# Moving more of the expert tiles and nine output groups into the main loop, and normalising the late groups on VectorE alone

## The reference

```python
x = x + gnn(layernorm(x), adj)       # 8192 rows of 128, adj 8192 x 8192
x = x + moe(layernorm(x))            # 16 experts, the best 2 of each row

def gnn(z, dist):                    # cutoff 1, mu 1, sigma 0.5
    weights = where(dist < 1, exp(-(1/dist - 1)**2 / 0.5), 0)
    return weights @ (z @ W + B)

def moe(x):
    topk_vals, topk_idx = top_k(x @ gate_w + gate_b, 2)
    share = softmax(topk_vals)
    expert_e(x) = relu(x @ w1[e] + b1[e]) @ w2[e] + b2[e]    # 128 -> 256 -> 128
    y = x + share[0] * expert_top1(x) + share[1] * expert_top2(x)
    return layernorm(y) * gamma + beta
```

## Time and profile before

| | before |
|---|---|
| median of three runs | 1727.93 us (1727.41 to 1729.02) |
| the profiled execution | 1725.96 us, its span 1724.2 us |
| busy, share of the span | PE 93%, ACT 91%, DVE 87%, POOL 31% |
| mean granted TensorE clock | 0.977 |
| first start of L720 in group 8 / 9 / 13 / 14 / 15 | 745.4 / 840.0 / 1243.0 / 1345.4 / 1453.6 us |
| last start of L720 (step 511) | 1553.4 us |
| last product of the tail | 1671 us |

### The profile page before, as it was taken

The page is one execution under the profiler, slowest core; times in us unless marked ns, Lnnn a source line. Parts: engine busy times, 40 slices in busy tenths (PEclk is TensorE's granted clock), DMA queues, the critical chain, the costliest instruction groups (busy, mean ns, idle before and its releaser), DMA issues.

```text
span 1724.2 us, 24880 instructions
## 1 busy us (share of the span) xinstructions
PE 1605.5 (93%) x8327; PEld 1069.9 (62%) x8327; DVE 1494.9 (87%) x2312; ACT 1563.5 (91%) x1530; POOL 538.3 (31%) x354
## 2 busy tenths in 40 slices
PE   4999999999999999999999999999998998988870
PEld 3666666666666666656666666666665665757760
DVE  7999989898989898999787878878898898877676
ACT  5899999999999999999999999999997998966662
POOL 1001040404040404090303012040464655465773
PEclk9999999999999999999999999999999999999985
DMA  9558976766666766676777777777776886735662
GB/s 322 150 159 261 259 215 204 207 201 209 201 208 202 208 201 208 200 219 199 216 222 222 216 217 208 220 216 222 226 216 189 239 234 200 228 101 148 183 180 82
DMA packets 246236, 354.26 MB, mean 205 GB/s; under 512 B 20896, under 2 KB 103584, under 8 KB 245984
## 3 DMA queue, kind: packets, MB, share of 16 engines
q1 hardware_dynamic: 237792, 335.62, 66.5%
q0 software_dynamic: 8320, 17.06, 3.2%
HBM read 318.99 MB, written 35.73 MB: 206 GB/s over the span
## 4 chain that ended last, share of the span: by engine, by line
PE 73%; DVE 14%; POOL 4%; issue 4%; ACT 2%; DMA 2%; SPq 1%; DVEq 0%; ACTq 0%; POOLq 0%
PE acc L1394 42%; PE tp L1464 21%; DVE chunk L864 4%; POOL early_back L633 4%; DVE chunk L870 3%; PE tp L1440 2%; PE tp L1431 2%; DVE stats L876 1%; PE tp L1491 1%; DVE chunk L1278 1%; PE acc L1508 1%; ACT chunk L824 1%; PE tp L1508 1%; PE misc L1370 1%; DVE msg L939 1%
## 5 line engine op out<-in xcount | busy, mean ns | idle before, releaser
L1394 PE MATMUL acc<-wT,msg 128*128 128x512 f32 x2048 | 974.3, 598 | 1.8 <-DVE yT L970 1.8
L720 ACT ACTIVATE wT<-tp 128x1024 f32<-128x1024 f32 x512 | 636.4, 1326 | 35.8 <-PE tp L1464 35.7
L870 DVE SCALAR_TENSOR_TENSOR chunk<-chunk 128x2048 f32<-128x2048 f32 x256 | 584.2, 2282 | 31.2 <-ACT chunk L713 30.8
L1464 PEld LDWEIGHTS tp<-ident,chunk 128*128 128x128 f32 x4096 | 478.6, 142 | 204.9 <-issue 199.0
L864 DVE SCALAR_TENSOR_TENSOR chunk<-chunk 128x2048 f32<-128x2048 f32 x256 | 583.7, 2281 | 2.0 <-DMA chunk<-in_adj_dram 2.0
L713 ACT ACTIVATE chunk<-chunk 128x2048 f32<-128x2048 f32 x256 | 567.7, 2217 | 0.1
L1464 PE MATMUL tp<-ident,chunk 128*128 128x128 f32 x4096 | 536.7, 274 | 9.5 <-DVE pair_out L1170 8.7
L1394 PEld LDWEIGHTS acc<-wT,msg 128*128 128x128 f32 x2048 | 351.4, 192 | 255.3 <-issue 249.9
L708 ACT ACTIVATE chunk<-chunk 128x4096 f32<-128x4096 f32 x118 | 466.3, 3951 | 2.3 <-DVE chunk L864 2.3
L673 POOL DMA_INDIRECT rows_in<-y,row_now x128 | 254.4, 1988 | 37.3 <-issue 37.3
L607 POOL TENSOR_TENSOR pool_carrier<-pool_carrier 1x1 f32<-1x1 f32 x32 | 29.8, 931 | 720.7 <-DVE row_now L1055 705.0
(11 more groups left out here) (143 smaller groups left out, 940.7 us busy)
## 6 DMA issues: line engine op xcount, KB each, us to landing
chunk<-in_adj_dram SPq DMA_DIRECT2D x256, 1024.0 KB, 5.7
pair_w<-first_layers SPq DMA_DIRECT2D x104, 129.0 KB, 5.1
pair_in<-rows_in SPq DMA_DIRECT2D x104, 64.0 KB
rows_out<-pair_out SPq DMA_DIRECT2D x52, 128.0 KB, 5.8
chunk<-rows_in SPq DMA_DIRECT2D x85, 64.0 KB
rows_out<-chunk SPq DMA_DIRECT2D x41, 128.0 KB
y_kept<-y SPq DMA_DIRECT2D x16, 256.0 KB, 6.1
rows_in<-zeros SPq DMA_DIRECT2D x64, 64.0 KB
```

What stands on the lines that cost most here:

```text
L720: act.activation(wT[:, s % WSLOTS, :], tp[place(s) % TSLOTS][:, :], ACT.Exp, scale=-2.0).then_inc(weighted, 1)
L870: dve.scalar_tensor_tensor(out=slot(c), in0=slot(c), scalar=2.0, in1=slot(c), op0=ALU.subtract, op1=ALU.mult).then_inc(squared, 1)
L1394: ins = pe.matmul(acc[:, :], msg[:, n, :], wT[:, (g * PPG + m) % WSLOTS, k * ROWS:(k + 1) * ROWS], start=(n == 0), stop=(n == 2 * PPG - 1))
L1464: ins = pe.transpose(tp[place(s) % TSLOTS][:, t * ROWS + b * P:t * ROWS + (b + 1) * P], chunk[:, c % RING, b, j:j + P], ident[:, :])
```

## The change

- All 128 units of batches 0 and 1 (batch 1 is padded from 55 to 56) run in the loop as 64 pairs. A slot comes after every second step: 38 slots from step 272 to 346, and 30 from step 432 to 490.
- 62 units are left for the tail. They start at iteration 16 (UNIT_AT), where the tables of batch 2 exist; their rows are loaded from iteration 7 on (ROWS_AT). In the iterations before, only the gate of group 15, the table and an early group run.
- Nine groups are early instead of five, at EARLY_AT = 369, 378, 400, 409, 431, 440, 463, 503, 509. The last two belong to batch 1. The gather buffer is split into three halves of four gathers each, each with a semaphore of its own; a half is freed as soon as it is summed. The guess moves from GpSimd to ScalarE, five steps after EARLY_AT; refining and the first normalising pass share one slot.
- Seven groups are late instead of eleven, starting at iterations 20, 31, 52, 66, 76, 86, 96. Their normalisation is two passes of four instructions each on VectorE (subtract the mean and times gamma; times the inverse root plus the residual). ScalarE's four instructions, the `shift`, and two waits between the engines go. A late group takes eight iterations instead of eleven.
- `ones` and `before`, used only at the start, now live in `early_back`.

```diff
-    SLOT_EVERY = 4
-    PAIR_FIRST = [0, UNITS[0] // 2]
-    SECOND_PAIRS = 16
-    NP = PAIR_FIRST[1] + SECOND_PAIRS
+    IN_LOOP = 2
+    SLOT_EVERY = 2
+    PAIR_FIRST = [UNIT0[b] // 2 for b in range(IN_LOOP)]
+    NP = UNIT0[IN_LOOP] // 2
-    AT_STEP = [(FIRST[b + 1] + 1) * PPG + 21 for b in range(2)]
+    AT_STEP = [(FIRST[b + 1] + 1) * PPG + 16 for b in range(IN_LOOP)]
+    SLOT_STEP = [AT_STEP[b] + SLOT_EVERY * i for b in range(IN_LOOP) for i in range(UNITS[b] // 2 + 2)]
+    ROWS_STEP = [SLOT_STEP[n] - 7 if p < 3 or p - 3 < PAIR_FIRST[pair_batch(p)] else SLOT_STEP[n - 3] + 1
+                 for p, n in enumerate(TURN_SLOT)]
+    WEIGHTS_STEP = [SLOT_STEP[n] - 1 for n in TURN_SLOT]
...
-    EARLY_AT = (436, 461, 471, 493, 503)
-    EARLY_GATE = (12, 13, 13, 14, 14)
+    EARLY_AT = (369, 378, 400, 409, 431, 440, 463, 503, 509)
+    EARLY_GATE = (10, 10, 11, 11, 12, 12, 13, 14, 14)
+    EARLY_HALVES = 3
...
-        COMBINE_LONG = 11
+        UNIT_AT = 16
+        ROWS_AT = 7
+        COMBINE_LONG = 8
+        starts = dict(zip(LATE, (20, 31, 52, 66, 76, 86, 96)))
...
             def gather_early(h):
+                b = max(b for b in range(len(BATCHES)) if FIRST[b] <= h)
+                for k in range(K):
+                    q = K * h + k
+                    last_carried()
+                    if h == FIRST[b] and k == 0:
+                        results_there(b)
+                        pool.wait_ge(idx_ready, b + 1)
+                    if q >= EARLY_HALVES:
+                        pool.wait_ge(early_free, q - EARLY_HALVES + 1)
+                    carry()
+                    for t in range(TB):
+                        gather(h, b, k * TB + t, early_back[:, q % EARLY_HALVES, t, :], early_rows[q % EARLY_HALVES])
...
+            def guess_early(h):
+                act.wait_ge(early_moments, h + 1)
+                act.activation(early_lnv[:, :], early_mv[:, :, 1], ACT.Ln, bias=eps[:, 0:1]).then_inc(early_lnv_ready, 1)
+                act.wait_ge(early_lnv_ready, h + 1)
+                act.activation(early_rs[:, :], early_lnv[:, :], ACT.Exp, scale=-0.5).then_inc(early_guessed, 1)
...
                 if m == 6:
                     need()
-                    dve.scalar_tensor_tensor(out=shift[:, i, :], in0=mv_now[:, i, :, 0], scalar=-1.0, in1=rs[:, i, :],
-                                             op0=ALU.mult, op1=ALU.mult).then_inc(rs_ready, 1)
-                if m == 8:
-                    dve.wait_ge(zn_ready, h + 1)
-                    done(dve.tensor_tensor(z, z, gamma_bc[:, :].unsqueeze(1).to_broadcast([P, TB, D]), ALU.mult))
-                if m == 9:
+                    for b in range(TB):
+                        ins = dve.scalar_tensor_tensor(out=z[:, b, :], in0=z[:, b, :], scalar=mv_now[:, i, b, 0:1],
+                                                       in1=gamma_bc[:, :], op0=ALU.subtract, op1=ALU.mult)
+                    done(ins)
+                if m == 7:
                     need()
                     if h >= FIN:
                         dve.wait_ge(stored[h % FIN], h // FIN * 16)
-                    dve.tensor_tensor(fin[h % FIN], z, rows(xs, g), ALU.add).then_inc(fin_ready, 1)
+                    for b in range(TB):
+                        ins = dve.scalar_tensor_tensor(out=fin[h % FIN][:, b, :], in0=z[:, b, :], scalar=rs[:, i, b:b + 1],
+                                                       in1=rows(xs, g)[:, b, :], op0=ALU.mult, op1=ALU.add)
+                    ins.then_inc(fin_ready, 1)
```

More of the change, by code:

```diff
@@ L194, in gnn_moe_kernel @@
         pair_out = sb("pair_out", [P, 2, 2, D])
-        early_back = sb("early_back", [P, KB, D])
+        early_back = sb("early_back", [P, EARLY_HALVES, TB, D])
+        ones, before = early_back[:, 0, 0, :], early_back[:, 0, 1, :]
         early_z = sb("early_z", [P, 2, TB, D])
@@ L307, in gnn_moe_kernel @@
         pair_stored = [sem(f"pair_stored{i}") for i in range(2)]
-        early_rows = sem("early_rows")
+        early_rows = [sem(f"early_rows{i}") for i in range(EARLY_HALVES)]
         early_free = sem("early_free")
@@ L551, in _ @@
             for i in range(LAST + 2):
[L552 to L555, removed]
+                if 0 <= i - UNIT_AT - 1 < NT:
+                    store_rows(i - UNIT_AT - 1)
+                if i == ROWS_AT:
+                    for v in range(RIN):
+                        load_rows(v)
+                if RIN <= i - UNIT_AT + RIN < NT:
+                    load_rows(i - UNIT_AT + RIN)
                 if i == 11:
@@ L664, in gather_late @@
                 carry()
-                gather(g, b, back[h % BACK], back_in[h % BACK])
+                for kb in range(KB):
+                    gather(g, b, kb, back[h % BACK][:, kb, :], back_in[h % BACK])
             def scatter(g):
@@ L681, in _ @@
                         gather_early(h)
-                        guess_early(h)
                 if g == GROUPS - 1:
-                    for late in range(EARLY, FIRST[1]):
-                        gather_late(late)
+                    gather_late(EARLY)
+                    gather_late(EARLY + 1)
                 scatter(g)
-            for g in range(FIRST[1], GROUPS):
+            for g in range(EARLY + 2, GROUPS):
                 gather_late(g)
@@ L796, in _ @@
                         pair_slot(SLOT_AFTER[g * PPG + m])
+                    for h in range(EARLY):
+                        if g * PPG + m == EARLY_AT[h] + 5:
+                            guess_early(h)
             def copy_rows(u):
@@ L1512, in _ @@
             assert BEHIND == 2 and T_BANKS == 2 and TURN_LEAD == 4 and HIDDEN_LEAD == 2
-            turn_tile(0)
-            turn_tile(1)
             products(GROUPS - 1, PPG - 2)
-            turn_tile(2)
-            turn_tile(3)
-            hidden(0)
             products(GROUPS - 1, PPG - 1)
-            hidden(1)
-            for i in range(max(NT, PPG)):
-                if i + TURN_LEAD < NT:
-                    turn_tile(i + TURN_LEAD)
-                if i + HIDDEN_LEAD < NT:
-                    hidden(i + HIDDEN_LEAD)
-                if i < NT:
-                    output(i)
+            for i in range(UNIT_AT + NT):
+                if 0 <= i - UNIT_AT + TURN_LEAD < NT:
+                    turn_tile(i - UNIT_AT + TURN_LEAD)
+                if 0 <= i - UNIT_AT + HIDDEN_LEAD < NT:
+                    hidden(i - UNIT_AT + HIDDEN_LEAD)
+                if 0 <= i - UNIT_AT < NT:
+                    output(i - UNIT_AT)
                 gate_slot(GROUPS - 1, i)
```

113 lines of the change are left out of this document (36 added, 77 removed).

## The result

The changed kernel took **1737.15 us** (median of 5 runs, 1734.48 to 1742.14); the kernel before took 1727.93 (1726.12 to 1729.02, 5 runs). The ratio is 1.0056, 95% interval 1.004 to 1.0072: **slower by 0.4 to 0.7%**. Forecast were 1721 and faster.

A forecast was written before the change was run, and what follows sets the result against it. TensorE was taken to bound steps with pair work, ScalarE those without. Terms +27 - 21.5 + 23 + 3 - 38 = -6.5 us took the profiled 1725.96 to 1719.5; with 2.0 for the median, 1721, range 1698 to 1741.

The forecast's parts named there:

- rival D: Pair ranges of the loop: slots every two steps don't hold 7.2 us, costing 20 us, 1741; chance 0.08.
- Part 1: Loop steps 256 to 511: 64 pairs, a slot every second step, TensorE staying the bound; +27 us.
- Part 2: Groups 13 to 15: VectorE's old waits for late gathered rows of early groups go; -21.5 us.
- Part 3: Steps 369 to 427, no pairs: VectorE's excess from four early groups and a table 17.8, late gathers 5; +23 us.
- Part 5: Tail after the last exponential: 133 us against 170.8, bounds 123 and 144; -38 us.
- Part 4: Other early groups, at 431, 440, 463 among pairs and 503, 509 at the loop's end; +3 us (0 to 8).
- Rival C: Steps 389 to 432: GpSimd starved beside the table, gathers for 400, 409, 431 late; up to 13 us more, 1734; chance 0.18.
- B: Rival: VectorE's excess mostly absorbed in steps without pairs, or tail at its lower bound; 1706, with both 1698; chance 0.20.
- E: Rival: the tail's gain goes into its starting hole and GpSimd's serial gathers; tail 144 us, 1732; chance 0.12.

The follow-up runs named there:

- e0: The changed kernel run again unaltered, as base on the experiments' chip: 1735.45 us, 1.0037 of the kernel before.
- e2: Changed kernel without the gathers of the first six early groups and the waits for them, VectorE's sums reading other rows: 1721.52 us, ratio 0.9961.
- e4: Changed kernel with only GpSimd's order altered: four of an early group's eight gathers ahead of the guesses of groups 10, 11 and 12: 1722.15 us, ratio 0.9969.
- e3: Changed kernel keeping all gathers and waits, without VectorE's and ScalarE's arithmetic for the first six early groups: 1717.93 us, ratio 0.994.
- e7: Changed kernel with two instead of four early groups in the steps without pairs, GpSimd's gathers ordered half by half: 1706.7 us, ratio 0.9876.
- e8: Same as e7, with the ninth early group's slots starting at place 520 instead of 509: 1706.02 us, ratio 0.9869.

## Why the prediction was wrong

It had 1721, faster; it became 1737.15, slower, on the side that had 0.28. That it lies inside the range (1698 to 1741) is luck: the range reached that far for rival D, which did not happen. Term by term, with the measured numbers of the first profile, and of e0 where it differs:

| step | predicted | measured |
|---|---|---|
| Part 1, 64 pairs | +27 | +30 |
| Part 2, the old early stalls | −21.5 | −21.5 |
| Part 3, VectorE's excess | +17.8 | +20.4 |
| Parts 3 and 4, GpSimd's gathers late | +5, +3 | +21.0 (e0: +13.5) |
| Part 5, the tail | −38 | −33.9 |
| sum | −6.5 | +16.0 (e0: +8.4) |
| span, to 1724.2 before | | +16.2 (e0: +9.5) |

Where the measured column comes from. Part 1: steps 256 to 351 take 335.7 us in both; by the prediction's prices they are 21 x 2.69 + 75 x 2.65 + 36 x 2.00 = 327.2, and 5.5 for the table: 332.7. The 3.0 above this are Part 1's, put on its 27. Steps 432 to the last are 266.0 in e2, and 266.2 by the prices (59 x 2.65 + 28 x 2.00 + 20 x 2.69). Part 2: groups 14 and 15 above run with TensorE full, and group 13's loss is counted in the rows after, so the row keeps the forecast's own number. The tail is 136.9 or 136.8 against 170.8. The sum falls 1.1 us short of the spans' difference in e0 and 0.2 in the first profile.

**Part 3 is the step that failed, in its term for GpSimd: "I take 5 us of VectorE's waits for it".** It was 13.5 to 21 with Part 4's three, 5.5 to 13 more than forecast, the largest miss of all. e4 shows that this lateness decides the sign: it changes nothing else and lies at 0.9969. But it isn't the whole error. Part 1 was 3.0 too low, VectorE's excess 2.6 and the tail 4.1. With the gathers no later than forecast, these alone bring the sum from -6.5 to about +3, no gain either; with them as forecast, e0's 13.5 alone would bring it to -1. In e0 it took both.

**Rival C is what happened**, in kind. Its price of up to 13 us more was reached in the first profile; in e0 it was 5.5, less than the 10 that it set as the line for itself, and the other misses carried the time over 1731.4. Its mechanism was off in place. I had tied the starvation to the table of batch 1 and looked for it at the early groups of 400, 409 and 431. The long waits stood at steps 370, 401 and 431 (5.75, 8.73 and 7.45 us): at the early group that comes first behind each guess, with or without a table. The earlier trace rows had led me there, since both its rows stand beside a table. The trace of before also holds a batch behind a table (it ended at 1278), GpSimd before, in order of time:

```profile
1281.13 3.58 POOL L607 TENSOR_TENSOR pool_carrier<-pool_carrier 1x1 f32<-1x1 f32 x1 [15.53 <-DMA rows_out<-pair_out]
...
1286.29 7.03 POOL L633 DMA_INDIRECT early_back<-rows_out,row_back  x1 [0.30 <-issue]
```

I had read the earlier trace rows instead, where no gather took over 3.5 us. The mean of its scatter, 2.94, already hid two that took 5.40 and 6.69. The length of a batch was forecast rightly: 20 to 30 us for eight gathers, and 28.6 lies inside. What failed is what it was held against, the 24 us between two slots. What counts is when a batch's last half lands. The guess of group 10 begins near step 358 and the one of group 11 near 390; it and eight gathers take 34 to 35 us here, thirteen steps, and the slots they serve lie at 369 and 400, eleven and ten steps on.

**VectorE's excess** was right in mechanism and 2.6 too small. A part of it shows an interlock that I hadn't seen. TensorE after, in order of time, at the start of group 13, and VectorE there:

```profile
1278.42 1.88 PE L1387 MATMUL acc<-wT,msg 128*128 128x512 f32 x4
1288.41 3.75 PE L1387 MATMUL acc<-wT,msg 128*128 128x512 f32 x4 [6.87 <-DVE yT L962]
```

```profile
1285.42 1.07 DVE L1101 TENSOR_REDUCE unit_e<-work 1x56 f32<-1x896 f32 x1
1286.52 1.14 DVE L1207 SCALAR_TENSOR_TENSOR early_z<-early_z,early_rs,xs 128x128 f32<-128x128 f32 x4
1287.58 0.68 DVE L962 COPY yT<-acc 128x512 f32<-128x512 f32 x1
```

The first product of a group overwrites the accumulator, so it waits for VectorE's copy of the last group's. The copy stood behind the table and the early group of step 409, and TensorE waited 6.87 us for it. The lead that VectorE has ends there, once a group; it can't be carried past a group's start. So the 20.4 us are four early groups and the table, and 6.9 of them fall at 416 because the table and the early group at 409 stand in one place. e3, without early sums, and e7, with neither early group of 400 and 409 in the gap, have 2.68 us a step there.

**Part 1** held: slots every second step work (rival D is out), with TensorE busy 117.41 of 117.7 us against 116.8 by the prices. **Part 2** held. Of the signs the prediction named, steps 272 to 346 took 3.63 us each (3.6 forecast), steps 369 to 431 3.24 (e0 3.13; 3.1 forecast), the waits ahead of `early_z` there were 21.9 us (under 8), and the last exponential began at 1603.5 (1585).

**Part 5** was 4 us short, all of it at the start: the first output came 23.7 us after the last exponential, not 19.5; the results of batch 2 were stored at +83 instead of +79; and the rest went as written. The carrier that waits for them, GpSimd after:

```profile
1686.49 0.18 POOL L601 TENSOR_TENSOR pool_carrier<-pool_carrier 1x1 f32<-1x1 f32 x1 [25.25 <-DMA rows_out<-chunk]
```

TensorE at the start of the tail, after:

```profile
1609.35 0.65 PE L1353 MATMUL misc<-ident,yT 128*128 128x128 f32 x4 [0.79 <-DVE yT L962]
1620.06 1.12 PE L1324 MATMUL misc<-ident,y 128*128 128x128 f32 x4 [10.05 <-DVE y L983]
...
1624.21 1.06 PE L1484 MATMUL tp<-msg,chunk 128*128 128x128 f32 x4
...
1628.72 0.61 PE L1484 MATMUL tp<-msg,chunk 128*128 128x128 f32 x4
```

VectorE had the unit table (L1120) at 1617.1, 13.7 us after the last exponential and not 11. TensorE stood for 10 us before 1620, and its first units ran at the lower of its two clocks, 1.2 GHz: from 1620 to 1627 the granted clock was 0.50, and four products took 1.06 us instead of the 0.61 that they take from 1627 on, at 1.00 or 2.4 GHz. The granted clock of both stretches together, after, with L1484's own busy time:

```profile
1620.00:1640.00 20.00, 9.82 (x56) 8.74 (x56) 0.82 0.60 169
```

So 2.7 of the 4.2 us are the later table, and the rest is the way through load, units and lower clock, which I did not take apart. In e8 the table was there at +10.5, and the gain went into another wait: VectorE's sums for the moved early group stood ahead of `yT`, and TensorE waited 4.36 us more for that (e8, in order of time):

```profile
1579.76 1.12 PE L1329 MATMUL misc<-ident,y 128*128 128x128 f32 x4 [6.88 <-DVE y L988]
...
1585.66 1.89 PE L1368 MATMUL misc<-gws,yT 128*128 128x16 f32 x8 [4.36 <-DVE yT L994]
```

Of the rivals, B did not happen; E did in kind (137 us of its 144), and alone it would not have decided. Three slips in the prediction's sums are small beside all this: the 7.45 above for 7.1; 1.6 us for a unit in 1610 to 1627, where ten units in 17.0 us are 1.7, 1.2 us over its twelve; and B with both of its conditions, 1721 - 15 - 10, is 1696 and not 1698.

## What to carry to other kernels

A queue that hands out rows must be judged by when the last row of a batch lands, from where the batch starts and from its slowest instructions, and not from the mean and the distance between two users. Put early what only needs its inputs: four gathers moved ahead of one short computation in GpSimd's program, in three places, were worth 12 to 13 us and turned a loss into a gain, with no work taken away. And work for a second engine is cheap only where the bounding engine has something longer to do than that engine: moved among the pairs, an early group cost under 1 us. In the gap it depends on how much else is there: the first two and the table cost 5.4 us together (0.3 of them in group 11), a third early group 6.6 and a fourth, beside the table, 8.6.

## What the runs showed of the hardware

GpSimd's instructions, even the smallest, can take several us longer while VectorE runs masks and squares back to back. VectorE after, in order of time, beside the two long ones that ended at 1116.99 and 1124.03:

```profile
1113.89 2.29 DVE L862 SCALAR_TENSOR_TENSOR chunk<-chunk 128x2048 f32<-128x2048 f32 x1
1116.10 0.69 DVE L989 COPY yT<-misc 128x512 f32<-128x512 f32 x1
1116.70 2.28 DVE L856 SCALAR_TENSOR_TENSOR chunk<-chunk 128x2048 f32<-128x2048 f32 x1
...
1123.90 0.22 DVE L998 TENSOR_TENSOR logits<-misc,gb_bc 128x64 f32<-128x64 f32 x1
```

Both held instructions ended one usual duration after VectorE began an instruction that reads `misc`, in PSUM: 1116.10 + 0.94 = 1117.0, and 1123.90 + 0.18 = 1124.1. Between these two VectorE ran only masks, squares and one TENSOR_TENSOR on `xs`. The two long rows of before, above, fit as well: VectorE's two instructions on `misc` began there at 1284.58 and 1292.39, and the held ones ended at 1284.71 and 1293.32. It may be why long ones stand behind a guess so often: the guess lets VectorE make `y`, and the copy and the logits follow it. But it isn't a rule. GpSimd before, in order of time, inside a scatter:

```profile
1249.85 11.78 POOL L673 DMA_INDIRECT rows_in<-y,row_now  x1 [0.30 <-issue]
```

VectorE began an instruction that reads `misc` at 1257.83 (L978) and this DMA went on; it ended 0.9 us after VectorE began one with its only input in SBUF (L876, at 1260.72). Nor do all long ones follow a guess: in e4 one of 11.41 us stands ahead of the guess of group 12, at 1278.20.

The Trainium skill ("SBUF — State Buffer", the section on the two separate sides) says that VectorE with two inputs in SBUF and a GpSimd operation that reads SBUF exclude each other: whichever starts first has the shared ports for its whole instruction, and the other waits. The trace agrees and adds that the hold can last over three or four such instructions in a row, 6.8 to 7.0 us in the rows above. What lets GpSimd in between two of them at other times (the gather at 1103.57 ended at 1106.52, in the middle of a mask) stays open; no run here takes that apart, and the instructions on `misc` are what was seen beside these ends, not a cause shown.
